# Triangular solve's scalings on VectorE, the root's product in another bank, and another order in the last slots

## The chip, the cores and the metric

The program runs on one core of one Trainium2 chip. TensorE multiplies matrices, VectorE, ScalarE and GpSimd work element by element, and SyncE issues transfers. The engines run side by side, each in its own order, and wait for one another on semaphores. The metric is device time in microseconds, lower is better. The kernel before took 1187.59 us, the median of three runs (1184.17, 1188.15, 1187.59).

## The reference

One decoder layer on 32 sequences of 64 tokens, 256 wide: a gated delta-rule attention over 128 steps per sequence (two keys for each token, 8 heads of 128), a cross attention with 16 heads and a window of 8 keys, and a gated feed-forward net of 1024 with weights stored as integers. After each comes a layer norm of the sum.

```
x = layernorm(x + delta_attention(x))      # 8 heads, T = 2 * 64 steps
x = layernorm(x + cross_attention(x, ctx, seg_id))
x = layernorm(x + ffn(x))                  # weights (w_int - 128) * scale

def step(state, inp):                      # the delta rule
    q_t, k_t, v_t, g_t, b_t = inp
    state = state * exp(g_t)
    corr = einsum('bhk,bhkv->bhv', k_t, state)
    v_new = (v_t - corr) * b_t
    state = state + einsum('bhk,bhv->bhkv', k_t, v_new)
    return state, einsum('bhk,bhkv->bhv', q_t, state)
o = o * rsqrt(mean(o * o) + EPS) * o_norm_w * silu(gg)
```

The kernel does not step through the 128 states. It builds the matrix of decayed products of the keys and solves a unit triangular system, in blocks of 32 rows.

## The kernel before

**Two phases.** `delta_phase` computes the first attention up to the gated heads; `tile_phase` does everything behind it, on 16 tiles of 128 tokens. Each engine has one program, written out in its order of execution; nothing reorders it.

**The delta phase** has 32 units (a head and a group of 8 sequences; U = 32) and runs in slots s = 0 to 42. It is a pipeline: slot s projects and convolves keys and queries of unit s, V and the gate of unit s - 9 (LAG = 9), makes the output of unit s - 10 and norms unit s - 11. From slot 32 on no new keys come; from slot 37 on parts of the tile phase stand between the slots' own work (`ahead[...]`), `last_slot` is 40.

**The solve** goes in 8 batches of 4 units (NS = 4). VectorE loads the 32x32 blocks (`solve_load`, `solve_norms`), GpSimd scales the rows by rho (L1396), runs 30 elimination steps of two instructions each (`eliminate`, L1328 and L1331), sets the diagonal and scales the columns (L1400, L1402), and VectorE turns the result (`solve_turn`, L1161, and `solve_turn_again`, L1165). The steps are cut up over four slots by the tables CUTS and LAST_CUTS: each slot has three pieces, ahead of and behind W_scaled and at the slot's end. X is the tile called `inverse`, rank_one the product of a step. The last batch, number 7, is eliminated in slots 33 to 36, and slot 37 is the first to need it.

**A slot's chain.** TensorE: `chain_y` (L628), V's first projection, the root's product `norm` (L724), `chain_inverse_low` (L638), `turn_v` (L534), V's second projection, the chain's high and low products (L664, L666; L651, L687 apart in the last slots), the gate's projection, `chain_sum_low` (L677), `output` (L552). ScalarE copies W (L947), GpSimd multiplies it by the key's norms (W_scaled, L1426), and `output` needs that. `less_sum` (L1191) on VectorE follows `chain_sum_low`; the next `chain_y` needs it. `norm` writes the mean of squares into bank VB, and `turn_v` writes V turned into the same bank; ScalarE takes the logarithm and the exponential (L989, L992).

**The seam.** The first tiles' work: `out` (w_out, L1571), first norm (`sums`, `normalize`: L1811 to L1818, L1839), `turn_x1` (L1580), query products, `scores` (L1620) with the turned queries that SyncE moves 16 pieces at a time (L1535), softmax (L1853 to L1864), `attT` (L1656), the mix with kvtok (L1678), ctxT copies (L1775) and w_uvo (L1691), second norm, `ffn` (L1632), down product (L1701). w_up is unpacked on VectorE (L1886), w_down on GpSimd (L1936, L1938). `span` runs s = 2 to 19, with tile u1 = s in its first part, s - 1 in scores, s - 2 in the cross attention's end, s - 3 in the feed-forward net and s - 4 in the last norm.

## Time and profile before

| | |
|---|---|
| profiled execution | 1185.69 us, span 1183.9 us, mean granted clock of TensorE 0.987 |
| busy | TensorE 1118.0 (94%), VectorE 819.6 (69%), ScalarE 704.7 (60%), GpSimd 517.7 (44%) |
| chain that ended last | TensorE 74%, VectorE 9%, GpSimd 7%, ScalarE 4% |

| stretch, us | TensorE busy | VectorE | ScalarE | GpSimd | granted clock |
|---|---|---|---|---|---|
| 620 to 640 (slot 33) | 14.19 | 12.57 | 10.81 | 11.07 | 0.83 |
| 640 to 660 | 19.22 | 14.57 | 17.60 | 16.31 | 1.00 |
| 660 to 680 (slots 36, 37) | 16.09 | 13.01 | 13.99 | 14.94 | 0.98 |
| 760 to 780 | 15.09 | 12.21 | 10.91 | 7.75 | 0.91 |
| 780 to 800 (the seam) | 15.79 | 15.24 | 4.76 | 5.92 | 0.91 |
| 800 to 1130 (steady tiles) | 329.14 | 199.21 | 147.59 | 32.50 | 1.00 |

A stretch's busy time is read against its length: 20 us in all rows but the last, 330 there. The granted clock is the share of TensorE's full 2.4 GHz; 0.5 is 1.2 GHz. Slots 33 to 37 start on TensorE at 617.8, 636.0, 649.1, 662.2 and 677.6 us.

### The profile page before, as it was taken

The page shows a single profiled execution, that of the slowest core. Times are in us where ns is not written, and L with a number is a line of the kernel's source. Part 1 is how long each engine was busy: PE and PEld are TensorE (multiplying, and loading weights), DVE is VectorE, ACT ScalarE, POOL GpSimd, SP SyncE. Part 2 cuts the span into 40 slices and gives each one's busy share as a digit, 9 for nine tenths or more (in the row PEclk, how much of TensorE's full clock was granted, in tenths as well). Part 3 has the DMA queues.
Part 4 walks back from the last instruction along what each step waited for, and adds up shares of the span by engine and source line. Part 5 has one row for each costly group of instructions (what it writes and reads, how often), then busy time and mean ns, then how long its engine had stood idle before and what let it go on. Part 6 is the DMA issues. An engine that isn't in the chain of part 4 may idle for free.

```text
span 1183.9 us, 28721 instructions
## 1 busy us (share of the span) xinstructions
PE 1118.0 (94%) x11460; PEld 772.8 (65%) x11460; DVE 819.6 (69%) x1447; ACT 704.7 (60%) x1214; POOL 517.7 (44%) x717
## 2 busy tenths in 40 slices
PE   8887899999999999999998899879999999999997
PEld 3444455555555555555555566668999899989976
DVE  5997778868868778779776655666556666565552
ACT  5776567777676776776766766534443444444443
POOL 1659486585784883983976712241100000010000
PEclk9999899999999999999998999989999999999999
DMA  4223234555545454565645542331222211112100
GB/s 122 49 51 81 69 51 79 87 106 74 115 79 92 95 78 89 113 123 116 127 75 167 160 129 64 113 102 46 50 51 52 68 52 46 46 45 51 30 16 9
DMA packets 147284, 93.74 MB, mean 79 GB/s; under 512 B 80688, under 2 KB 130736, under 8 KB 146256
## 3 DMA queue, kind: packets, MB, share of 16 engines
q1 hardware_dynamic: 146000, 91.71, 35.2%
q8 instruction: 91, 1.49, 0.5%
q14 instruction: 41, 0.34, 0.1%
q10 hardware_dynamic: 1152, 0.21, 0.1%
HBM read 54.77 MB, written 14.55 MB: 59 GB/s over the span
## 4 chain that ended last, share of the span: by engine, by line
PE 74%; DVE 9%; POOL 7%; ACT 4%; issue 3%; SPq 1%; DMA 1%; ACTq 0%; DVEq 0%; POOLq 0%
PE proj L528 21%; PE out L1632 5%; PE turned_v_chain L1632 5%; PE gram L543 5%; PE turned_v_chain L1701 4%; PE proj L1691 4%; PE proj L1571 4%; DVE conv L1114 3%; POOL inverse L1331 3%; PE gram L1606 2%; POOL rank_one L1328 2%; PE out L552 2%; PE turned_v_chain L534 2%; PE decays L559 2%; PE turned_v_chain L677 1%
## 5 line engine op out<-in xcount | busy, mean ns | idle before, releaser
L1114 DVE SCALAR_TENSOR_TENSOR conv<-proj,kq_weights,conv 128x504 f32<-128x504 f32 (+2 forms) x261 | 189.7, 732 | 30.4 <-ACT conv L843 24.0
L528 PE MATMUL proj<-xT,vg_weights 128*128 128x512 f32 x384 | 190.9, 621 | 2.2 <-DVE conv L1114 2.0
L1930 POOL TENSOR_TENSOR rope<-rope_part,rope_part 128x512 f32<-128x512 f32 x32 | 40.0, 1271 | 319.1 <-DVE rope_part L1871 319.1
L1114 DVE SCALAR_TENSOR_TENSOR conv<-proj,vg_weights,conv 128x504 f32<-128x504 f32 (+2 forms) x192 | 140.7, 733 | 45.2 <-ACT conv L843 40.1
L528 PE MATMUL proj<-xT,kq_weights 128*128 128x512 f32 x348 | 167.6, 608 | 0.2 <-DVE conv L1114 0.2
L1331 POOL TENSOR_TENSOR inverse<-inverse,rank_one 128x30 f32<-128x30 f32 (+14 forms) x240 | 126.5, 527 | 18.8
L1328 POOL TENSOR_TENSOR rank_one<-inverse 128x30 f32<-128x30 f32 (+14 forms) x240 | 116.8, 487 | 15.0
L528 PEld LDWEIGHTS proj<-xT,vg_weights 128*128 128x128 f32 x384 | 68.9, 193 | 66.5 <-issue 60.4
L528 PEld LDWEIGHTS proj<-xT,kq_weights 128*128 128x128 f32 x348 | 62.7, 191 | 74.8 <-issue 69.1
L843 ACT ACTIVATE conv<-proj,kq_weights 128x512 f32<-128x512 f32 x87 | 59.6, 687 | 54.6 <-PE proj L528 54.4
L1710 ACT ACTIVATE rstd<-rstd 128x1 f32<-128x1 f32 x48 | 9.7, 202 | 136.1 <-DVE rstd L1818 136.1
L543 PEld LDWEIGHTS gram<-keys_q 128*64 128x64 f32 x896 | 56.8, 136 | 51.8 <-ACT keys_q L854 33.5
L543 PE MATMUL gram<-keys_q 128*64 128x160 f32 (+2 forms) x896 | 73.4, 293 | 9.4 <-ACT keys_q L854 9.4
L854 ACT ACTIVATE keys_q<-conv 128x512 f32<-128x512 f32 x96 | 63.4, 667 | 16.9 <-DVE conv L1114 16.2
L843 ACT ACTIVATE conv<-proj,vg_weights 128x512 f32<-128x512 f32 x64 | 43.9, 685 | 41.7 <-PE proj L528 41.5
L1691 PE MATMUL proj<-t_w_uvo,ctxT 128*128 128x256 f32 x256 | 59.4, 386 | 2.7 <-ACT ctxT L1775 2.7
L1426 POOL TENSOR_TENSOR W_scaled<-W,k_norm 128x512 f32<-128x512 f32 x32 | 35.3, 1104 | 54.6 <-ACT W L947 54.6
L1701 PE MATMUL turned_v_chain<-t_w_down,hid 128*128 128x256 f32 x256 | 58.0, 379 | 0.9 <-DVE hid L1878 0.9
L1435 POOL TENSOR_TENSOR o_sum<-o_sum,q_sq 128x512 f32<-128x512 f32 x23 | 29.5, 1283 | 64.2 <-ACT o_sum L1046 64.2
L1176 DVE COPY Y<-turned_v_chain 32x256 f32<-32x256 f32 x64 | 27.1, 424 | 41.1 <-PE turned_v_chain L628 39.6
L1691 PEld LDWEIGHTS proj<-t_w_uvo,ctxT 128*128 128x128 f32 x256 | 48.5, 194 | 9.7 <-issue 3.5
L1701 PEld LDWEIGHTS turned_v_chain<-t_w_down,hid 128*128 128x128 f32 x256 | 48.6, 190 | 7.7 <-DVE hid L1878 1.1
(257 smaller groups left out, 2487.6 us busy)
## 6 DMA issues: line engine op xcount, KB each, us to landing
kq_weights<-in_kq_w SPq DMA_DIRECT2D x32, 390.0 KB, 6.5
vg_weights<-in_vg_w SPq DMA_DIRECT2D x32, 390.0 KB, 6.2
o_scratch<-oT SPq DMA_DIRECT2D x32, 256.0 KB, 2.2
o_in<-o_scratch SPq DMA_DIRECT2D x16, 512.0 KB, 4.0
o_rs<-o_rs_quarters SPq DMA_DIRECT2D x88, 64.0 KB, 6.1
diagonal<-gram_decayed SPq DMA_DIRECT2D x128, 32.0 KB, 1.9
inverse<-inverse SPq DMA_DIRECT2D x32, 128.0 KB, 2.8
q_first<-rope SPq DMA_DIRECT2D x128, 32.0 KB, 1.9
```

The lines of the kernel that those rows point to most:

```text
L528: mm = e.matmul(bank(c, u)[:], w[:, (k * 3 + c % 3) * 128:(k * 3 + c % 3 + 1) * 128], xT[g][:, k, :], start=(k == 0), stop=(k == KD - 1))
L543: mm = e.matmul(out[p, b % 4, cols], kq[:, b, S:][:, p], kq[:, b, cols], start=True, stop=True)
L843: e.activation(acc(c, u)[:], bank(c, u)[:].rearrange("p (b l) -> p b l", l=S), ACT.Copy, scale=weights(c, u)[:, j:j + 1]).then_inc(s_tap[c ...
L854: e.activation(out, acc(c, u)[:], ACT.Silu).then_inc(s_silu[c], 1)
L1114: e.scalar_tensor_tensor(acc(c, u)[:, :, back:], src[:, :, 0:S - back], weights(c, u)[:, j:j + 1], acc(c, u)[:, :, back:], ALU.mult, ALU.a ...
L1328: e.tensor_tensor(product, X[:, k + 1:, k:k + 1].broadcast_to([128, n, k]), X[:, k:k + 1, 0:k].broadcast_to([128, n, k]), ALU.mult).then_i ...
L1331: e.tensor_tensor(X[:, k + 1:, 0:k], X[:, k + 1:, 0:k], product, ALU.add).then_inc(s_elim, 1)
L1571: mm = e.matmul(out_bank(u)[:, 0:D], o_in[u % 2][:, h, :], w_out[:, h, :], start=(h == 0), stop=(h == H - 1))
L1632: mm = e.matmul(ffn_bank[r][:, (2 * i + j) * TILE:(2 * i + j + 1) * TILE], wt[:, k, (2 * r + j) * 128:(2 * r + j + 1) * 128], x2T[:, k, :] ...
L1691: mm = e.matmul(b0[:, 0:D], ctxT[:, hp].rearrange("p b q -> p (b q)"), w_uvo[:, hp, :], start=(hp == 0), stop=(hp == XH // 2 - 1))
L1701: mm = e.matmul(b6[:, 0:D], hid[:, k, :], w_down[:, k, :], start=(k == 0), stop=(k == FJ - 1))
L1930: e.tensor_tensor(turned[half][:].rearrange("p b r q -> p r b q"), parts[2 * half][:], parts[2 * half + 1][:], op).then_inc(s_turned, 1)
```

## The change

In the delta phase: (1) the last batch's rows are scaled by VectorE, right behind its norms in slot 33, and its columns (with the memset of the diagonal) by VectorE in slot 36, right ahead of `solve_turn`. (2) GpSimd takes W_scaled first in slots 32 to 36 and the steps behind it, in pieces of 11, 8 and 11 (LAST_CUTS); batch 6's column scaling too comes behind W_scaled in slot 32. (3) For units 22 to 29 the root's product goes into bank P[1], which the second projections of V use: `norm` waits for the convolution that read it, V's projection for the logarithm, and `turn_v` no longer.

In the tile phase: (4) each transfer of integers has a semaphore of its own, w_up is unpacked ahead of the second norm of tile 0, w_down by VectorE in one instruction in the next step, instead of two on GpSimd. (5) At the seam (u3 == 0) ScalarE copies ctxT ahead of the queries and VectorE does tile 1's softmax sum behind the second norm. (6) In the last slots ScalarE copies x2T ahead of the last norm's root. (7) The down product starts when three of hid's four parts are there and waits for the fourth ahead of its seventh of eight pieces.

```diff
-LAST_CUTS = (((1, 1), (5, 13), (1, 5)), ((13, 13), (13, 21), (21, 21)), ((21, 21), (21, 31), (31, 31)), ((31, 31), (31, 31), (31, 31)))
+LAST_CUTS = ((1, 12), (12, 20), (20, 31), (31, 31))
...
+        in_v_bank = lambda u: by_rows(u) or u + LAG + 2 > last_slot
...
                     else:
-                        mm = e.matmul(VB, ones_mean[:], o_sum[:], start=True, stop=True)
+                        if not in_v_bank(u):
+                            e.wait_ge(s_conv[V1], 3 * (u + 2))
+                        mm = e.matmul(VB if in_v_bank(u) else P[1][:], ones_mean[:], o_sum[:], start=True, stop=True)
                     mm.then_inc(s_norm, 1)
...
                     if live(ud):
                         e.wait_ge(s_silu[V1], ud + 1)
-                        wait(e, s_ln, ud)
+                        if in_v_bank(ud - 1):
+                            wait(e, s_ln, ud)
...
                             e.wait_ge(s_conv[Q], 3 * (ub + 1))
                         else:
                             e.wait_ge(s_conv[V1], 3 * uc)
+                        if not in_v_bank(uc - 2):
+                            e.wait_ge(s_ln, uc - 1)
                         project(V1, uc)
...
                             e.wait_ge(s_gr, uo)
-                            o_ln, o_mean = o_rs[:], VB
+                            o_ln, o_mean = o_rs[:], VB if in_v_bank(uo) else P[1][:]
                         e.activation(o_ln, o_mean, ACT.Ln, scale=float(2 ** O_SHIFT), bias=guard[:, 0:1]).then_inc(s_ln, 1)
...
 
+                def solve_scale_rows(h):
+                    e.wait_ge(s_solve, SOLVE * h + READY)
+                    e.tensor_tensor(X, X, rho[:, :, None].broadcast_to([128, RB, RB]), ALU.mult).then_inc(s_elim, 1)
+
+                def solve_scale_columns(h):
+                    e.wait_ge(s_elim, ELIM * h + ELIM - 2)
+                    e.memset(padded[:, 0:RB * RB:RB + 1], 1.0).then_inc(s_elim, 1)
+                    e.wait_ge(s_elim, ELIM * h + ELIM - 1)
+                    e.tensor_tensor(X, X, rho[:, None, :].broadcast_to([128, RB, RB]), ALU.mult).then_inc(s_elim, 1)
...
                         solve_norms(loading)
+                        solve_scale_rows(loading)
...
                     if turning is not None and s > U:
+                        solve_scale_columns(turning)
                         solve_turn(turning)
...
                     solving = 0 <= h < NB_SOLVE
-                    cuts = (LAST_CUTS if h == NB_SOLVE - 1 else CUTS)[cut]
+                    cuts = ((1, 1), LAST_CUTS[cut], (1, 1)) if h == NB_SOLVE - 1 else CUTS[cut]
...
                     elif solving:
-                        if cut == 0 and s > U:
-                            scale_rows()
-                            eliminate(h, cuts[2])
                         eliminate(h, cuts[0])
-                        if cut == 3 and s <= U:
+                        if cut == 3 and s < U:
                             scale_columns()
                     if live(ud):
...
                                         ALU.mult).then_inc(s_wk, 1)
                     if solving and h > 0:
                         eliminate(h, cuts[1])
-                        if cut == 3 and s > U:
+                        if cut == 3 and s == U:
                             scale_columns()
                     if live(ud) and s <= U:
...
                         e.tensor_tensor(oT[uo % 2][:], oT[uo % 2][:], o_rs[:], ALU.mult).then_inc(s_gr, 1)
-                    if solving and h > 0 and not (cut == 0 and s > U):
-                        if cut == 0:
+                    if solving and h > 0:
+                        if cut == 0 and s < U:
                             scale_rows()
                         eliminate(h, cuts[2])
...
                             mm.then_inc(s_cross, 1)
                         if live(u4):
-                            e.wait_ge(s_hid, 4 * (u4 + 1))
+                            e.wait_ge(s_hid, 4 * u4 + 3)
                             if u4 == 0:
-                                e.wait_ge(s_down_w, 2)
+                                e.wait_ge(s_down_w, 1)
                             wait(e, s_parts, 4 * (u1 + 1) if live(u1) else 0)
                             wait(e, s_norm[2], 5 * u4 - 4)
                             for k in range(FJ):
+                                if k == FJ - 2:
+                                    e.wait_ge(s_hid, 4 * (u4 + 1))
                                 mm = e.matmul(b6[:, 0:D], hid[:, k, :], w_down[:, k, :], start=(k == 0), stop=(k == FJ - 1))
                             mm.then_inc(s_down, 1)
...
                         u1, u2, u3, u4, u5 = s, s - 1, s - 2, s - 3, s - 4
-                        if live(u5):
+                        if live(u5) and live(u1):
...
                             e.activation(x2T[:], b5[:, 0:KD * TILE].rearrange("p (k n) -> p k n", k=KD), ACT.Copy).then_inc(s_x2tout, 1)
+                        if live(u5) and not live(u1):
+                            rsqrt(2, u5)
                         if live(u1):
                             copy_x1(u1)
...
-                        if live(u1):
+                        if live(u1) and u3 != 0:
                             copy_nope(u1)
...
                             e.wait_ge(s_mix, u3 + 1)
                             wait(e, s_cross, u3)
                             for b, bk in enumerate((b1, b2)):
                                 e.activation(ctxT[:, :, b, :], bk.rearrange("p (h q) -> p h q", q=S), ACT.Copy).then_inc(s_ctx, 1)
+                        if u3 == 0:
+                            copy_nope(u1)
                         if live(u4):
...
                     if n == "w_up":
-                        e.wait_ge(done["ints"], 32)
+                        e.wait_ge(done["up"], 16)
...
+
+                def unpack_down():
+                    e.wait_ge(done["scales"], 64)
+                    e.wait_ge(done["down"], 16)
+                    e.scalar_tensor_tensor(w_down[:], ints["w_down"][:], -ZERO_POINT, scales["w_down"][:, None, :].broadcast_to([128, FJ, D]),
+                                           ALU.add, ALU.mult).then_inc(s_down_w, 1)
...
+                        if s == AHEAD:
+                            dequantize("w_up")
+                        if s == AHEAD + 1:
+                            unpack_down()
                         if live(u4):
                             hidden(2, u4)
                             hidden(3, u4)
...
-                        if live(u2):
+                        if live(u2) and u3 != 0:
                             softmax_sum(u2)
                         if u3 == 0:
                             e.wait_ge(done["scaled"], U)
                         if live(u3):
                             sums(1, u3)
                             normalize(1, u3)
-                        if s == AHEAD:
-                            dequantize("w_up")
+                        if u3 == 0:
+                            softmax_sum(u2)
                         if live(u1):
...
-                def unpack_down():
-                    e.wait_ge(done["scales"], 64)
-                    e.wait_ge(done["ints"], 32)
-                    e.tensor_scalar(w_down[:], ints["w_down"][:], -ZERO_POINT, None, ALU.add).then_inc(s_down_w, 1)
```

GpSimd, slots 32 and 33, from behind batch 6's last step (`inverse` is the solve's tile). Before:

```order
L1400 MEMSET inverse 128x32
L1402 TENSOR_TENSOR inverse<-inverse,rho 128x1024
L1426 TENSOR_TENSOR W_scaled<-W_125,k_norm_143 128x512
L1435 TENSOR_TENSOR o_sum<-o_sum,q_sq_113 128x512
L1442 TENSOR_TENSOR oT_145<-oT_145,o_rs 128x512
L1396 TENSOR_TENSOR inverse<-inverse,rho 128x1024
L1328 TENSOR_TENSOR rank_one<-inverse 128x30
L1331 TENSOR_TENSOR inverse<-inverse,rank_one 128x30
```

After:

```order
L1441 TENSOR_TENSOR W_scaled<-W_125,k_norm_143 128x512
L1418 MEMSET inverse 128x32
L1420 TENSOR_TENSOR inverse<-inverse,rho 128x1024
L1450 TENSOR_TENSOR o_sum<-o_sum,q_sq_113 128x512
L1457 TENSOR_TENSOR oT_145<-oT_145,o_rs 128x512
L1441 TENSOR_TENSOR W_scaled<-W_126,k_norm_143 128x512
L1346 TENSOR_TENSOR rank_one<-inverse 128x30
L1349 TENSOR_TENSOR inverse<-inverse,rank_one 128x30
```

W_scaled of both slots has moved up, ahead of the column scaling and ahead of the last batch's first step; the row scaling has left GpSimd.

VectorE, slot 33, from the end of the last batch's norms to the sum of squares (`kq_decayed` is less_sum's, `oT` first gate_output's, then scale_output's). Before:

```order
L1154 MEMSET inverse 128x16
L1114 SCALAR_TENSOR_TENSOR conv_87<-proj,vg_weights_84,conv_87 128x8x63
L1114 SCALAR_TENSOR_TENSOR conv_87<-proj,vg_weights_84,conv_87 128x8x62
L1114 SCALAR_TENSOR_TENSOR conv_87<-proj,vg_weights_84,conv_87 128x8x61
L1249 SCALAR_TENSOR_TENSOR oT_144<-out,o_norm_w,gate_132 128x512
L1186 TENSOR_TENSOR oT_144<-oT_144,o_rs 128x512
L1191 TENSOR_TENSOR kq_decayed_71<-kq_decayed_71,turned_v_chain 64x8x32
L1181 TENSOR_TENSOR o_sum<-o_sum,q_sq_114 128x512
```

After:

```order
L1160 MEMSET inverse 128x16
L1164 TENSOR_TENSOR inverse<-inverse,rho 128x1024
L1120 SCALAR_TENSOR_TENSOR conv_87<-proj,vg_weights_84,conv_87 128x8x63
L1120 SCALAR_TENSOR_TENSOR conv_87<-proj,vg_weights_84,conv_87 128x8x62
L1120 SCALAR_TENSOR_TENSOR conv_87<-proj,vg_weights_84,conv_87 128x8x61
L1265 SCALAR_TENSOR_TENSOR oT_144<-out,o_norm_w,gate_132 128x512
L1202 TENSOR_TENSOR oT_144<-oT_144,o_rs 128x512
L1207 TENSOR_TENSOR kq_decayed_71<-kq_decayed_71,turned_v_chain 64x8x32
L1197 TENSOR_TENSOR o_sum<-o_sum,q_sq_114 128x512
```

One instruction of 128x1024 has come in, and all that follows stands behind it.

VectorE at the seam, from the last of rope_parts(2) to the unpacking of w_up or the masks (`total` is softmax_sum(1), `res`, `stats`, `mv`, `rstd` and `x` the second norm of tile 0). Before:

```order
L1871 TENSOR_TENSOR rope_part_200<-proj,t_cos_149 128x512
L1860 TENSOR_REDUCE total<-att_206 128x16
L1862 RECIPROCAL total<-total 128x16
L1864 TENSOR_TENSOR att_206<-att_206,total 128x1024
L1811 TENSOR_TENSOR res_184<-proj,x_0_175 128x256
L1813 BN_STATS stats_187<-res_184 128x6
L1815 BN_AGGR mv_190<-stats_187 128x2
L1818 TENSOR_SCALAR rstd_193<-mv_190 128x1
L1839 TENSOR_SCALAR x_0_178<-res_184,mv_190,rstd_193 128x256
L1886 SCALAR_TENSOR_TENSOR t_w_up<-w_up_ints,w_up_scale 128x1024 x2
L1800 TENSOR_TENSOR mask_173<-t_keys,seg 128x128
```

After:

```order
L1892 TENSOR_TENSOR rope_part_200<-proj,t_cos_149 128x512
L1907 SCALAR_TENSOR_TENSOR t_w_up<-w_up_ints,w_up_scale 128x1024 x2
L1832 TENSOR_TENSOR res_184<-proj,x_0_175 128x256
L1834 BN_STATS stats_187<-res_184 128x6
L1836 BN_AGGR mv_190<-stats_187 128x2
L1839 TENSOR_SCALAR rstd_193<-mv_190 128x1
L1860 TENSOR_SCALAR x_0_178<-res_184,mv_190,rstd_193 128x256
L1881 TENSOR_REDUCE total<-att_206 128x16
L1883 RECIPROCAL total<-total 128x16
L1885 TENSOR_TENSOR att_206<-att_206,total 128x1024
L1821 TENSOR_TENSOR mask_173<-t_keys,seg 128x128
```

w_up's unpacking has moved from behind the second norm to ahead of it, softmax_sum from ahead to behind.

## Rows read from the trace of the kernel before

**Rows 1.** Timeline of PE, slots 33 and 37: start, length (us), operation, idle before.
```profile
634.14 1.98 PE L552 MATMUL out<-W_scaled,V 128*64 128x64 f32 x32 [5.18 <-POOL W_scaled L1426]
...
677.57 0.69 PE L628 MATMUL turned_v_chain<-inverse,gram_decayed 32*32 32x32 f32 x32 [2.57 <-DVE inverse L1161]
```

**Rows 2.** Groups of POOL, 629.5 to 671.8 us: busy, mean ns | idle before.
```profile
L1331 POOL TENSOR_TENSOR inverse<-inverse,rank_one 128x30 f32<-128x30 f32 (+14 forms) x30 | 17.8, 593 | 2.4
L1328 POOL TENSOR_TENSOR rank_one<-inverse 128x30 f32<-128x30 f32 (+14 forms) x30 | 14.9, 498 | 2.1
L1426 POOL TENSOR_TENSOR W_scaled<-W,k_norm 128x512 f32<-128x512 f32 x4 | 4.2, 1041 | 2.0 <-ACT W L947 2.0
L1396 POOL TENSOR_TENSOR inverse<-inverse,rho 128x1024 f32<-128x1024 f32 x1 | 1.9, 1914 | 7.6 <-DVE inverse L1154 7.6
```

**Rows 3.** Timeline of POOL: the scaling of the columns, last batch.
```profile
672.87 2.60 POOL L1402 TENSOR_TENSOR inverse<-inverse,rho 128x1024 f32<-128x1024 f32 x1
```

**Rows 4.** Timeline of ACT: the copy of W in slot 32.
```profile
612.47 0.59 ACT L947 ACTIVATE W<-turned_v_chain 64x512 f32<-64x512 f32 x1
```

**Rows 5.** Timeline of DVE, slots 32 and 33.
```profile
614.99 2.05 DVE L1161 STREAM_TRANSPOSE inverse<-inverse 128x1024 f32<-128x1024 f32 x1
617.92 0.69 DVE L1127 TENSOR_TENSOR gram_decayed<-gram,decayed 128x512 f32<-128x512 f32 x1 [0.88 <-PE gram L543]
...
631.07 0.41 DVE L1191 TENSOR_TENSOR kq_decayed<-kq_decayed,turned_v_chain 64x256 f32<-64x256 f32 x1
```

**Rows 6.** Groups of DVE by shape: busy, mean ns | idle before.
```profile
L1864 DVE TENSOR_TENSOR att<-att,total 128x1024 f32<-128x1024 f32 x16 | 20.0, 1248 | 0.6
```

**Rows 7.** Queue of SyncE; DMA issues of 636 to 639 us (KB, us to landing).
```profile
638.14 0.39 SPq L449 DMA_DIRECT2D vg_weights<-in_vg_w  x1
...
vg_weights<-in_vg_w SPq DMA_DIRECT2D x1, 390.0 KB, 6.9
```

**Rows 8.** Waits, 600 to 830 us: us in total, times, longest.
```profile
PE turned_v_chain L534 <- ACT o_rs L989: 4.1, 8, 1.2
```

**Rows 9.** Timeline of PE at the seam, 775 to 792 us.
```profile
775.30 5.13 PE L1691 MATMUL proj<-t_w_uvo,ctxT 128*128 128x256 f32 x16 [2.66 <-ACT ctxT L1775]
...
784.80 0.69 PE L1620 MATMUL proj<-t_kE,q_first 128*64 128x64 f32 x16
...
791.59 0.47 PE L1580 MATMUL turned_v_chain<-ident,x 128*128 128x128 f32 x2 [3.46 <-DVE x L1839]
791.86 1.91 PE L1632 MATMUL out<-x2T,t_w_gate 128*128 128x128 f32 x8
```

**Rows 10.** Timeline of ACT at the seam: the first copy of ctxT.
```profile
774.11 0.60 ACT L1775 ACTIVATE ctxT<-proj 128x512 f32<-128x512 f32 x1
```

**Rows 11.** Tile q_second on SyncE: issue ns, first and last start, landing.
```profile
L1535 SPq DMA_DIRECT2D q_second<-rope x8: 596/597/602, 773.3 to 782.2; - x8
...
DMA to landing us min/median/max: 1.9/1.9/2.4
```

**Rows 12.** Timeline of DVE at the seam.
```profile
777.60 1.22 DVE L1860 TENSOR_REDUCE total<-att 128x16 f32<-128x1024 f32 x1 [5.25 <-ACT att L1734]
...
782.45 3.70 DVE L1839 TENSOR_SCALAR x<-res,mv,rstd 128x256 f32<-128x256 f32 x1 [0.51 <-ACT rstd L1712]
786.07 2.35 DVE L1886 SCALAR_TENSOR_TENSOR t_w_up<-w_up_ints,w_up_scale 128x1024 f32<-128x1024 int32 x2
```

**Rows 13.** Timeline of POOL at the seam.
```profile
781.47 4.53 POOL L1938 TENSOR_TENSOR t_w_down<-t_w_down,w_down_scale 128x2048 f32<-128x2048 f32 x1
```

**Rows 14.** Waits, 1100 to 1184 us.
```profile
PE out L1632 <- ACT x2T L1752: 2.5, 2, 1.9
...
PE turned_v_chain L1701 <- DVE hid L1878: 0.9, 1, 0.9
```

**Rows 15.** Timeline of PE: L1606 with a wait inside it, and without.
```profile
711.87 2.19 PE L1606 MATMUL gram<-qc,t_w_qn 96*128 96x128 f32 x16
...
769.66 1.95 PE L1606 MATMUL gram<-qc,t_w_qn 96*128 96x128 f32 x16
```

More of the change, by code:

```diff
@@ L244, in delta_phase @@
             "const", "in", "kv_stored", "stored", "rope_stored", "product", "copied", "rope"))
-        d_w, d_ints, d_uvo, s_wgt = sem("d_weights"), sem("d_ints"), sem("d_w_uvo"), sem("ffn_weights")
+        d_w, d_up, d_down, d_uvo, s_wgt = sem("d_weights"), sem("d_up"), sem("d_down"), sem("d_w_uvo"), sem("ffn_weights")
         d_gate = sem("d_gate_weights")
@@ L412, in weights_after_chain @@
                     e.dma_start(tiles["w_uvo"][:], scratch["w_uvo"]).then_inc(d_uvo, 16)
-                    for n, k in (("w_up", "up"), ("w_down", "down")):
-                        e.dma_start(ints[n][:].rearrange("p k n -> p (k n)"), a[f"{k}_w"]).then_inc(d_ints, 16)
+                    for n, k, landed in (("w_up", "up", d_up), ("w_down", "down", d_down)):
+                        e.dma_start(ints[n][:].rearrange("p k n -> p (k n)"), a[f"{k}_w"]).then_inc(landed, 16)
                 def gate_weights():
@@ L1455, in delta_phase @@
     tiles["ints"], tiles["scales"] = ints, scales
-    done = {"o": s_og, "w_high": s_whiout, "scaled": s_gr, "stored": d_out, "weights": d_w, "first": d_first, "uvo": d_uvo, "ffn": s_wgt, "ints": d_ints, "scales": d_gate, "decays": s_ee,
+    done = {"o": s_og, "w_high": s_whiout, "scaled": s_gr, "stored": d_out, "weights": d_w, "first": d_first, "uvo": d_uvo, "ffn": s_wgt, "up": d_up, "down": d_down, "scales": d_gate, "decays": s_ee,
             "gram": s_gm, "gate": s_silu[G], "v1": s_conv[V1], "high": s_wlo, "low": s_wloout, "solve": s_solve}
@@ L1931, in rope @@
                                         parts[2 * half + 1][:], op).then_inc(s_turned, 1)
-                def unpack_down():
-                    e.wait_ge(done["scales"], 64)
-                    e.wait_ge(done["ints"], 32)
-                    e.tensor_scalar(w_down[:], ints["w_down"][:], -ZERO_POINT, None, ALU.add).then_inc(s_down_w, 1)
-                    e.wait_ge(s_down_w, 1)
-                    e.tensor_tensor(w_down[:], w_down[:], scales["w_down"][:, None, :].broadcast_to([128, FJ, D]),
-                                    ALU.mult).then_inc(s_down_w, 1)
                 def loop():
```

2 lines of the change are left out of this document (removed).

## The prediction

> **What bounds the kernel now.** I read the page first: its busy digits put TensorE at nine tenths or more almost everywhere, and the chain that ended last is TensorE for 74%. From 800 us on, where the tiles run in a steady state, the matmuls leave no gap. So nothing in this change can help there; it can help only where TensorE stands still, and the list of waits and then the timelines say where that is. There are four such places, and all of them are touched.
>
> First, slots 33 to 37, the last batch of the triangular solve. In slot 33 TensorE waits 5.18 us in front of `output(23)` for GpSimd's W_scaled, and at the head of slot 37 2.57 us for the inverse that VectorE turns [rows 1]. These are one matter. GpSimd's queue holds the last batch's work in a row: the scaling of the rows (1.9 us), 60 elimination instructions (14.9 + 17.8 us busy and 2.4 + 2.1 us between them, 37.2 us together), four W_scaled of 1.04 us among them, one wait of 2.0 us for W [rows 2], and at the end the scaling of the columns, 2.6 us [rows 3]. That is 1.9 + 37.2 + 4.2 + 2.0 + 2.6 = 47.9 us, with 0.2 for a memset 48.1. TensorE's work in those slots is shorter than that, so this chain, not TensorE, sets the time at which slot 37 starts. The 5.18 us wait is not worth 5.18 us: it is slack against that chain.
>
> Second, the root's product in the bank of the turned V: turn_v waits for ScalarE's logarithm 8 times, 4.1 us in all [rows 8]. Third, the seam at 775 to 792 us: 2.66 us for ctxT and 3.46 us for x, with a matmul group at half clock behind each [rows 9]. Fourth, the last slots: 2.5 us for x2T and 0.9 us for hid [rows 14].
>
> **Term 1, the solve chain: 2.4 us.** Slot 32: W_scaled now stands in front of batch 6's column scaling. W is copied until 612.47 + 0.59 = 613.06 [rows 4], so W_scaled ends at 614.1 and memset and scaling (0.2 + 2.6) end at 616.9. VectorE's turn of the inverse moves from 614.99 to 616.9; it had 0.88 us to spare behind it [rows 5], so everything later on VectorE in slots 32 and 33, the loading of the last batch included, is 1.0 us late. TensorE no longer waits for W_scaled there, but then waits for the inverse, so that gain is not kept.
>
> Slot 33: the scaling of the rows moves to VectorE, right behind the norms. An operation of 128x1024 with both inputs in SBUF takes VectorE 1.25 us where nothing disturbs it [rows 6]. W_scaled(23) is ready at just that time and GpSimd, now idle, runs it. What happens when both want SBUF is to be seen at the seam: the normalization that starts at 782.45 on VectorE takes 3.70 us [rows 12] and ends with GpSimd's operation, 781.47 + 4.53 = 786.00 [rows 13]. So I count a hold of one whole W_scaled: 1.04 + 1.25 = 2.3 us until step 1 can start; without a hold it is 1.3. The same at the end: when step 30 is done GpSimd takes up W_scaled(26) at once, VectorE is held for 1.04, then needs 1.25 and 0.1 for the memset: 2.4 us instead of 2.8, or 1.4 without the hold.
>
> The Trainium skill (SBUF — State Buffer, "Who interferes with whom") says that a VectorE instruction with two SBUF inputs contends with a GpSimd instruction that reads SBUF, and that whichever starts first keeps the pair of ports for its whole length. By that rule both scalings are held, as counted; if only the form seen at the seam, with one tensor input, were held, the sum would be 2.1 us better. The trace agrees with the hold at the seam; for two tensor inputs of the scaling's size no row here settles it.
>
> The new chain: start 1.0 later, 2.3 for the rows, 37.2 of steps, only two W_scaled (24 and 25) inside it = 2.1, a wait for W, and 2.4 for the columns. The wait: `less_sum(24)` stands behind the row scaling on VectorE, at 631.07 before [rows 5], now at 631.1 + 1.0 + 2.3 = 634.4, and `chain_y(25)`, the head of slot 34, needs it. TensorE would have reached output(23) at 634.14 - 5.18 = 629.0 [rows 1]; 1.0 later and with the product's 1.1 it is at chain_y at about 631, so the 5.18 us wait comes back as some 3.6 us in front of chain_y. Slot 34 then starts at 634.8, against 634.14 + 1.9 = 636.0 before. W(24) had kept GpSimd waiting for 2.0 us [rows 2] when it stood behind twelve steps; it comes 1.2 us earlier now, the eleven steps ahead of it end about as late as eleven steps did before, and W_scaled(23), 1.04, has left the queue: estimated, W(24) is some 0.7 us late. Sum: 1.0 + 2.3 + 37.2 + 2.1 + 0.7 + 2.4 = 45.7, against 48.1: 2.4 us. On SyncE the store of unit 22's output waits for VectorE's scale_output, which is as late as less_sum; behind it stand nine loads and then the weights of unit 26, issued at 638.14 and landed 6.9 us later [rows 7]. Now that is 641.4 and 648.3; slot 35, one slot of 12 us behind 634.8, wants them at about 647.3. I count that within the 0.7. Bounds: no hold and no wait for W, 5.2 us; a wait for W of 3 us (late weights, TensorE at half clock), 0.
>
> **Term 2, the bank: 0.4 us.** The wait for the logarithm moves from turn_v(0) to `project(V1)`, one group of four transposes (some 0.5 us) later. At most that in each of 7 slots. But turn_v(1), behind V1, waits for ScalarE's copy of V, which comes after the same logarithm and its exponential: where the root waits were long (slots 38 to 40), V1 then ends earlier and TensorE waits for the copy instead. In slots 34 to 36 term 1's chain is the limit. I keep 0.2 us each in slots 37 and 39; bounds 0 and 2. `norm` gets a wait for V1's convolution of the slot before; in the order of VectorE's queue that is long done.
>
> **Term 3, the seam: 4.1 us.** ctxT's copies go ahead of the four copies of q. The product before ended at 775.30 - 2.66 = 772.64 [rows 9], the first copy started at 774.11 [rows 10]: 1.4 us earlier, so the w_uvo product ends at 780.4 - 1.4 = 779.0 or sooner. On VectorE w_up's unpacking (2.35 us [rows 12]) moves into its idle time before 777.60, where it waited 5.25 us; softmax_sum moves behind the second norm; GpSimd's two w_down operations are gone, and with them the hold (3.70 instead of about 0.4: 3.3 us). VectorE then: product end 779.0, second norm 2.4 (780.43 to 782.45 and the last operation), softmax_sum 2.7, mask and next first norm 3.2 (788.4 to 791.59): 787.3, when x1 is ready. TensorE: scores(2) need the stores of the turned queries; the last is issued at 782.2 and lands 1.9 later [rows 11], 784.1, and this path is not changed. From scores to turn_x1 it was 784.80 to 791.59 - 3.46 = 788.1, 3.3 us: 787.4. So turn_x1 at 787.5 instead of 791.59. Without the early w_uvo product the floor by TensorE's row stays the same; if VectorE is 1.5 late, 2.6 us are left; the stores cap it at 4.2. w_down's unpacking, 128x2048 in one operation, costs VectorE about 2.35 us (like w_up's two) in front of hidden(2), where VectorE otherwise waits for ScalarE: nothing. If that cover were gone, up to 2.35 us would be late in hidden(2), and by that the down product.
>
> **Term 4, the end: 3.1 us.** x2T goes ahead of the last root. Of 2.5 us of waits in two slots [rows 14], the longer, 1.9, keeps the copy itself, 0.4; the shorter is covered by the transposes of att: 2.1. The down product starts when three quarters of hid are there: the last one waits 0.9 us for the fourth, and six of its eight parts now fill that: 0.9; with the waits unrounded 3.1. Bounds 2.5 and 3.4.
>
> **Term 5, the clock: 1.7 us.** After the seam's 3.46 us wait the granted clock is the lower of its two levels: the first group of eight matmuls behind it takes 1.91 us [rows 9]. At the upper level half of that would do, and the next group is nearly as slow: some 1.7 us lost; behind the 2.57 us wait of slot 37 [rows 1] it fell too, and I count as much. The waits that I expect at these places are 1 to 1.5 us in slot 37 and some 2 us (for the stores) at the seam. I take one low stretch of two away: 1.7, bounds -1.7 (a new one, in slot 34 or 35) and 3.4.
>
> **The sum.** 2.4 + 0.4 + 4.1 + 3.1 + 1.7 = 11.7 us. The profiled execution took 1185.69 us (span 1183.9): 1174.0. The median of the runs is 1187.59, 1.9 above it: 1175.9, say 1176.
>
> **The rivals.**
> (a) The solve chain gives nothing back: late weights and a low clock in slot 34 put W(24) and W(25) behind the steps, and no low stretch vanishes. For it: four things are queued behind the row scaling on VectorE and SyncE. Against: the chain drops two W_scaled and a 2.0 us wait. 0.4 + 4.1 + 3.1 = 7.6 us less: 1180.0.
> (b) No hold on VectorE, no wait for W, both low stretches gone: 5.2 + 0.4 + 4.1 + 3.1 + 3.4 = 16.2 us less: 1171.4. Against it: GpSimd's W_scaled does coincide with both scalings.
> (c) Slower: the wait that now stands inside the down product, ahead of part 7 of 8, breaks TensorE's stream in each of 16 tiles, 13 of them steady. The trace has one such place: 16 matmuls with a wait in the middle took 2.19 us, without 1.95 [rows 15]. At 0.24 it costs 16 x 0.24 = 3.8, which leaves 7.9: 1179.7. It makes the kernel slower by over 0.3% from (11.7 + 3.6) / 16 = 0.96 us each; at 1.1 us each it is 17.6 - 11.7 = 5.9 us slower, 1193.5. For that, four times the only price seen would be needed.
> (d) The moved order only trades waits, slots 33 to 37 losing 4 by a longer chain and the seam gaining 1 because VectorE waits for w_up's load: 3.1 + 1 + 0.4 - 4 = 0.5 us less: 1187.1, within the noise.
>
> **Chances.** The forecast 0.54 (its own range 1173 to 1179), (a) 0.18, (b) 0.15, (c) at its small price 0.04 and at its large one 0.04, (d) 0.05. About 0.3% (3.6 us) is what a measurement of this kernel can tell from no change. Faster 0.91, same 0.05, slower 0.04. The range, 1170 to 1182, holds the forecast, nearly all of (b) and most of (a).
>
> **What would show it.** Term 1: W_scaled(23) right behind its W; a wait of 3 to 4 us at the head of slot 34 for less_sum; VectorE's scaling of 128x1024 at about 2.3 us rather than 1.25; slot 37 starting 2.4 us earlier. Term 3: x at 0.4 us, scores(2) waiting for q_second, turn_x1 some 4 us earlier relative to slot 42. Term 4: no wait for hid, x2T's wait 0.4. Term 5: one low stretch less. I am wrong if slot 37 starts over 5 us earlier or not earlier, or if a steady tile takes longer than before.

## The result and the profile after

The changed kernel takes 1176.84 us (median of 8 runs, 1172.62 to 1181.99), the kernel before 1186.37 (median of 8, its first three among them). The ratio is 0.9926, 95% interval 0.9902 to 0.9949. Timed again later it was 0.9923 (0.9911 to 0.9935). So it is faster by 9 us, in a range of 6 to 12. The profiled execution has a span of 1173.4 us, 10.5 less than before.

The stretches of the two programs are best compared by their own length, with these borders on TensorE: head of slot 32 (`chain_y(23)`), slot 37 (`chain_y(28)`), slot 38, the transposes of att of slot 41, where the seam begins, `down_q(3)` of the seam, and the last down product. First the kernel before (stretch in us, length, busy time and count of PE, PEld, DVE, ACT, POOL, mean granted clock, DMA share, GB/s):

```profile
602.74:677.59 74.85, 63.32 (x980) 39.66 (x976) 51.28 (x79) 54.15 (x87) 56.34 (x91) 0.95 0.55 147
677.59:696.40 18.81, 18.32 (x234) 11.30 (x234) 11.54 (x22) 9.54 (x16) 1.57 (x2) 0.91 0.66 185
696.40:764.77 68.37, 60.88 (x922) 43.48 (x921) 40.83 (x68) 45.11 (x76) 16.30 (x13) 1.00 0.22 58
764.77:795.28 30.51, 22.80 (x182) 19.05 (x180) 23.34 (x32) 10.17 (x19) 13.24 (x5) 0.89 0.46 162
795.28:1175.72 380.44, 375.26 (x3268) 338.26 (x3267) 218.88 (x472) 169.16 (x345) 32.50 (x26) 1.00 0.17 43
```

The same five stretches in the first profile of the changed kernel:

```profile
600.37:674.15 73.78, 65.09 (x978) 39.39 (x974) 53.81 (x82) 53.09 (x87) 51.80 (x88) 0.95 0.55 149
674.15:691.85 17.70, 16.67 (x232) 10.98 (x232) 12.40 (x22) 10.46 (x17) 2.31 (x3) 1.00 0.61 173
691.85:762.37 70.52, 64.18 (x921) 45.17 (x921) 41.83 (x68) 45.14 (x76) 17.19 (x13) 0.95 0.26 76
762.37:788.31 25.94, 20.93 (x182) 17.90 (x179) 19.72 (x31) 10.06 (x19) 3.49 (x2) 0.93 0.46 154
788.31:1165.33 377.02, 374.82 (x3268) 338.52 (x3267) 221.08 (x473) 168.58 (x344) 34.58 (x26) 1.00 0.17 44
```

The gains are 1.07, 1.11, -2.15, 4.57 and 3.42 us, and 2.37 come from ahead of slot 32 (602.74 against 600.37), where nothing was changed; together 10.4. The third stretch is longer although its waits are not: its clock is 0.95 where it was 1.00. 0.05 x 70.5 = 3.5 us of lost clock is one stretch of 7 us at half clock. The seam has less of it than before, 0.93 against 0.89. What belongs to the program and what to the execution can't be told from two profiles; the runs below tell part of it.

Slots 33 to 37 on TensorE, to be read beside [rows 1]:

```profile
630.98 1.16 PE L553 MATMUL out<-W_scaled,V 128*64 128x64 f32 x32 [2.38 <-DVE oT L1265]
...
671.00 1.15 PE L553 MATMUL out<-W_scaled,V 128*64 128x64 f32 x32 [1.82 <-POOL W_scaled L1441]
...
674.15 0.69 PE L629 MATMUL turned_v_chain<-inverse,gram_decayed 32*32 32x32 f32 x32 [0.99 <-DVE inverse L1177]
```

The wait of 5.18 us for W_scaled is 2.38 now, and it is for VectorE: `gate_output` stands behind the row scaling and the V1 convolution and frees the bank that `output(23)` writes. The size is this execution's; in the second profile of the same kernel the wait is 3.64 us. GpSimd in the same slots:

```profile
627.13 1.76 POOL L1441 TENSOR_TENSOR W_scaled<-W,k_norm 128x512 f32<-128x512 f32 x1 [10.30 <-ACT W L953]
...
643.17 1.52 POOL L1441 TENSOR_TENSOR W_scaled<-W,k_norm 128x512 f32<-128x512 f32 x1 [1.81 <-ACT W L953]
...
669.90 1.04 POOL L1441 TENSOR_TENSOR W_scaled<-W,k_norm 128x512 f32<-128x512 f32 x1
```

and VectorE's two scalings with the turn:

```profile
626.76 1.23 DVE L1164 TENSOR_TENSOR inverse<-inverse,rho 128x1024 f32<-128x1024 f32 x1
...
670.16 1.86 DVE L1170 TENSOR_TENSOR inverse<-inverse,rho 128x1024 f32<-128x1024 f32 x1
672.06 2.04 DVE L1177 STREAM_TRANSPOSE inverse<-inverse 128x1024 f32<-128x1024 f32 x1
```

The seam on TensorE answers to [rows 9]; the last line shows that the wait for x is gone:

```profile
771.30 3.69 PE L1706 MATMUL proj<-t_w_uvo,ctxT 128*128 128x256 f32 x16 [1.25 <-ACT ctxT L1794]
...
781.61 0.69 PE L1635 MATMUL proj<-t_kE,q_first 128*64 128x64 f32 x16 [2.29 <-DMA q_second<-rope]
...
786.31 0.38 PE L1595 MATMUL turned_v_chain<-ident,x 128*128 128x128 f32 x2
```

At the end, of the waits in [rows 14] one of 0.5 us is left, and hid is gone from the list:

```profile
PE out L1647 <- ACT x2T L1769: 0.5, 1, 0.5
```

### The profile page after: what moved, and what is told of

Read it like the earlier page. It is cut to its first block, busy times and chain, and to the rows that moved or that the text cites. A ratio compares the mean times of both kernels' runs of the same rounds, so it can differ in the third digit from the quotient of the medians.

```text
span 1173.4 us, 28728 instructions
## 1 busy us (share of the span) xinstructions
PE 1118.5 (95%) x11460; PEld 774.2 (66%) x11460; DVE 822.9 (70%) x1451; ACT 704.7 (60%) x1214; POOL 507.1 (43%) x712
## 4 chain that ended last, share of the span: by engine, by line
PE 76%; DVE 9%; POOL 5%; ACT 3%; issue 3%; SPq 2%; DMA 1%; ACTq 0%; DVEq 0%; POOLq 0%
PE proj L529 21%; PE out L1647 5%; PE gram L544 5%; PE turned_v_chain L1647 5%; PE turned_v_chain L1718 4%; PE proj L1706 4%; PE proj L1586 4%; DVE conv L1120 3%; PE gram L1621 2%; PE out L553 2%; PE turned_v_chain L535 2%; POOL inverse L1349 2%; PE decays L560 2%; POOL rank_one L1346 2%; SPq L1550 2%
## 5 line engine op out<-in xcount | busy, mean ns | idle before, releaser
L1120 DVE SCALAR_TENSOR_TENSOR conv<-proj,kq_weights,conv 128x504 f32<-128x504 f32 (+2 forms) x261 | 189.7, 732 | 30.1 <-ACT conv L849 23.7
L1961 POOL TENSOR_TENSOR rope<-rope_part,rope_part 128x512 f32<-128x512 f32 x32 | 43.1, 1367 | 324.7 <-DVE rope_part L1892 324.7
```

The costliest lines, as they stand in the source:

```text
L1120: e.scalar_tensor_tensor(acc(c, u)[:, :, back:], src[:, :, 0:S - back], weights(c, u)[:, j:j + 1], acc(c, u)[:, :, back:], ALU.mult, ALU.a ...
L1961: e.tensor_tensor(turned[half][:].rearrange("p b r q -> p r b q"), parts[2 * half][:], parts[2 * half + 1][:], op).then_inc(s_turned, 1)
```

## The experiments

Each ratio is taken against the kernel before on the same chip; e9 to e12 ran on another chip than e1 to e8. In the rows of stretches below the borders lie up to 0.7 us behind the named instructions, by the same amount at all borders of one profile, so the lengths are those from instruction to instruction.

**Each part of the change alone.** Four kernels, each the kernel before with one part of the diff and nothing else.

```diff
e1: -LAST_CUTS = (((1, 1), (5, 13), (1, 5)), ...   +LAST_CUTS = ((1, 12), (12, 20), (20, 31), (31, 31))
    +solve_scale_rows(loading)   +solve_scale_columns(turning)   (VectorE; gone from GpSimd)
e2: -e.matmul(VB, ones_mean[:], o_sum[:]   +e.matmul(VB if in_v_bank(u) else P[1][:], ...   (with its waits)
e3: +if u3 == 0: copy_nope(u1)   +if u3 == 0: softmax_sum(u2)   +unpack_down() on VectorE, w_up's earlier
e4: +if live(u5) and not live(u1): rsqrt(2, u5)   +if k == FJ - 2: e.wait_ge(s_hid, 4 * (u4 + 1))
```

> Before with only the last batch's part: both scalings on VectorE, GpSimd's steps behind the scaled W in cuts (1,12), (12,20), (20,31). My theory, read from the trace after: GpSimd's 30 steps stay one chain with one wait for W(24) inside (1.8 us) and the scaled W(26) ahead of the column scaling, so slot 37 starts only 1.1 us nearer to slot 32 than before, and slot 37 gets 1 us more by running at full clock: 2.2 us less in all, ratio 0.998. Rival, as I predicted: 2.4 from the chain and 1.7 from the clock, 4.1 less, 0.9965. Rival 2: nothing, the waits are only moved, 1.000.

> Before with only the root's product in P[1]. My theory: the wait for Ln goes, but the same turn waits for the V copy right behind it, so 0 to 0.4 us less: ratio 0.9997 to 1.000. Rival: the full gap of eight waits, 2 us less, 0.998.

> Before with only the seam's part: ctxT copied ahead of the copy, softmax_sum behind the normalizing, both feed-forward weights unpacked on VectorE in other places, two semaphores. My theory: mix to turn_x1(3) 2.7 us shorter and the feed-forward of tile 2 at full clock, 1.7: 4.4 less, ratio 0.9963. Rival: the wait for the unpacked w_down was hidden by the stores, 1 us less or nothing, 0.999.

> Before with only the end's part: x2T copied ahead of the root in the last slots, and the wait for the last quarter of hid inside the down product. My theory: 2.0 us of x2T's wait and 0.9 us of hid's at the end go, nothing is lost in the 15 steady tiles: 3 us less, ratio 0.9975. Rival: a wait inside the accumulation costs 0.24 us in each of 16 tiles, then 0.8 more, 1.0007.

Measured against before: e1 0.9986 (0.9971 to 1.0), e2 1.0004 (0.9992 to 1.0016), e3 0.9974 (0.9963 to 0.9984), e4 0.9957 (0.9942 to 0.9972). In us that is -1.7, +0.5, -3.1 and -5.1, in sum -9.4, as much as the whole change within the intervals. Clear of no change are the seam and the end; e1's interval ends at 1.0 and e2's holds it. The stretches show what each part does. Seam alone, fourth and fifth stretch:

```profile
765.00:791.13 26.13, 21.13 (x181) 17.87 (x180) 19.89 (x32) 10.35 (x20) 2.97 (x3) 0.93 0.53 183
791.13:1173.18 382.05, 376.88 (x3266) 339.86 (x3266) 221.15 (x473) 169.45 (x345) 34.60 (x26) 1.00 0.17 43
```

The seam is 4.4 us shorter than in the first profile of before, as in the whole change (but only 2.5 shorter than in the second, see below; the timed runs give 3.1); the tail of this execution lost 1.6 to a stretch at half clock at 1164. End alone, all stretches but the first:

```profile
678.05:695.19 17.14, 16.66 (x244) 10.96 (x238) 11.18 (x22) 9.92 (x16) 1.94 (x2) 1.00 0.63 189
695.19:765.99 70.80, 63.31 (x912) 45.11 (x905) 42.10 (x69) 44.77 (x76) 16.79 (x13) 0.95 0.27 75
765.99:793.43 27.44, 22.57 (x181) 18.47 (x180) 17.95 (x31) 10.37 (x20) 13.36 (x4) 0.88 0.42 141
793.43:1170.44 377.01, 374.82 (x3266) 338.23 (x3265) 219.48 (x472) 168.60 (x344) 32.53 (x26) 1.00 0.17 44
```

Its last stretch has the full 3.4 us of the end. But up to 793 us this kernel is the kernel before, and still slot 37 is 1.7 us shorter at full clock, the third stretch 2.4 longer and the seam 3.1 shorter at much the same clock. No edit did that. The bank alone makes the third stretch 68.09 instead of 68.37, 0.28 us, and slot 37 18.57 instead of 18.81, 0.24 us, and the timed runs see nothing of it. The solve part alone:

```profile
602.93:678.62 75.69, 64.87 (x986) 39.43 (x981) 55.90 (x83) 53.21 (x87) 50.98 (x88) 0.95 0.54 145
```

Slot 37 starts 0.84 us later against slot 32, not 1.1 earlier as I read from the trace after. The row scaling was held here (GpSimd's W_scaled kept it waiting), `output(23)` waited 3.64 us for VectorE, and a new wait stands behind it on TensorE:

```profile
650.21 2.62 PE L528 MATMUL proj<-xT,vg_weights 128*128 128x512 f32 x4 [1.70 <-DMA vg_weights<-in_vg_w]
```

with the load issued at 641.60 and 8.6 us on its way. The store of oT that SyncE has ahead of it waits for VectorE. GpSimd then waited 2.86 and 1.84 us for W(24) and W(25), in place of one wait of 2.0 [rows 2].

**The order in slots 33 and 34.** Four kernels on top of the change.

```diff
e5: -LAST_CUTS = ((1, 12), (12, 20), (20, 31), (31, 31))   +LAST_CUTS = ((1, 13), (13, 21), (21, 31), (31, 31))
e6: solve_scale_rows(loading); +gate_output(); +scale_output(uo); +less_sum(uc); convolve(V1, uc)
e7: SyncE: -if s == U + 1: weights_after_keys()   +the same in slot U + 2, behind the vg weights
e8: e6 and e7 together
```

> After with one more elimination step in slot 33, LAST_CUTS (1,13), (13,21), (21,31). My theory: GpSimd waits 1.8 us for W(24) in slot 34 with nothing in hand; a step of 1.3 us fits in there, so its chain and slot 37 come 1.0 to 1.3 us earlier against slot 32: ratio to before 0.9915 where after had 0.9926. Rival: the step makes the scaled W(24) late and TensorE loses what the chain gains, as after, 0.9926.

> After with gate_output, scale_output and less_sum directly behind the row scaling in slot 33, ahead of the V1 convolution. My theory: TensorE's wait for oT (2.38 us there) falls to under 0.5, chain_y(25) starts 1.5 to 2 us earlier, the store of oT and with it SP's queue too, so the weights of unit 26 land 1.5 us earlier, W(24) as well: slot 37 starts 1 to 2 us nearer to slot 32, ratio 0.9913. Rival: V1's convolution is late by the 1.8 us that was put ahead of it and the turned V of slot 34 waits for it: no change, 0.9926.

> After with SP's nine loads for the tile phase moved from slot 33 behind the load of the weights of unit 26 in slot 34. They are not wanted before slot 38. My theory: the late scaled oT holds SP's store and the eleven issues behind it; without them the weights are issued some 4.5 us earlier, TensorE's stop of 0.9 us at the head of slot 35 goes, slot 35 starts 0.9 earlier, and slot 37 gets part of it: 0.5 to 0.9 us, ratio 0.992. Rival: GpSimd's elimination alone sets slot 37, the stop of 0.9 goes but nothing is gained at slot 37, 0.9926.

> After with both of the last two edits. My theory: no stop of TensorE over 0.5 us from slot 33 to 35, and GpSimd waits for W(24) no more, since W comes 2 us earlier: its chain of 30 steps ends 1.5 to 2 us nearer to its start, slot 37 with it, ratio 0.991. Rival: GpSimd's chain is as long as before, whatever TensorE does, 0.9926.

Measured against before: e5 0.9916 (0.9899 to 0.9934), e6 0.9951 (0.9933 to 0.9969), e7 0.994 (0.9921 to 0.996), e8 0.9947 (0.9924 to 0.9971). From slot 32 to 37 they took 74.00, 76.32, 75.37 and 72.69 us (after 73.78). All four intervals against before overlap that of the changed kernel, so none of the four is shown to be faster or slower than it; what follows is read from the profiles. e5's theory, slot 37 1.0 us earlier, isn't borne out: `output(23)` waited 4.44 us for VectorE in this execution, W(24) came later by it, and the wait for it is still 1.75 us. e6's theory fell: the wait for oT became 1.47 us, and a stop of 2.74 us for the gate came, which ScalarE writes behind the V1 convolution that now ends later:

```profile
635.92 3.75 PE L529 MATMUL proj<-xT,vg_weights 128*128 128x512 f32 x4 [2.74 <-ACT gate L958]
```

So my rival was right in kind: VectorE is full in slot 33, and what goes first there makes something else late. e7's fell too: the weights are issued at 636.72 and land 3.7 us later instead of 7.5, yet the stop at the head of slot 35 is 0.70 us (0.93 and 0.66 in the two profiles of the changed kernel). Late weights were the wait in e1 but not that one; what it is stays open. e8's theory, no stop over 0.5 us and no wait for W(24), fell as well: TensorE stopped 2.54 us for the gate, and GpSimd waited 0.82 us. It is also a lesson in profiles: its profiled execution is the fastest of all (1172.09 us, clock 0.98 in the first stretch), and its median is 1180.65.

**Waits inside the product, a better order, and both kernels again.**

```diff
e9:  -e.wait_ge(s_hid, 4 * u4 + 3)      +e.wait_ge(s_hid, 4 * u4 + 1)
     -if k == FJ - 2: e.wait_ge(s_hid, 4 * (u4 + 1))
     +if k > 0 and k % 2 == 0: e.wait_ge(s_hid, 4 * u4 + k // 2 + 1)
e10: slot 33: +gate_output() ahead of solve_load(loading, 0); less_sum ahead of scale_output; and e7's edit
```

> After with the down product waiting for hid four times in each of the 16 tiles, ahead of its first, third, fifth and seventh step, where after waits ahead of the first and the seventh: 32 more waits inside the accumulation, and the two of them already fulfilled in the steady tiles. My theory: a wait that is already fulfilled costs nothing there; tile period 26.21 us as before, ratio as after, 0.9926. Rival: each costs 0.12 us or more, then 4 us more in all, 0.996, and a period of 26.45.

> After with gate_output of slot 33 ahead of the load of the diagonal (VectorE waits there 0.4 to 0.9 us for the DMA), less_sum ahead of scale_output, and SP's nine loads behind the weights of unit 26. My theory: output(23) waits for the scaled W alone, the V1 convolution is no later, chain_y(25) starts 1 to 1.4 us earlier against slot 32, and W(24) with it; slot 37 gets 1.0 to 1.4 us: ratio 0.9915. Rival: VectorE is full in slot 33 and TensorE stops for the gate behind the V1 convolution in place of oT; no gain, 0.9926.

> The changed kernel once more, unaltered, to see what a second profile and six more times of the same program show. My theory: the 2.3 us that its first profile was ahead of before already at 600 us are the run's, not the change's, so this profile is level with before there within 1 us, and the stretches at half clock lie elsewhere: span about 1176, ratio 0.9926 to 0.995. Rival: the lead ahead of slot 32 is the program's and stands here too, 2.3 us.

> The kernel before once more, unaltered, for a second profile of it. My theory: the number and the places of the half-clock stretches between 640 and 800 us differ from the first profile's, by one stretch of 3.4 us or more, although the program is the same. Rival: they lie in the same places, and what I saw move between kernels was moved by the edits. Ratio 1.000 either way.

Measured against before: e9 0.9941 (0.992 to 0.9962), e10 0.9911 (0.9898 to 0.9924), after again 0.9923, before again 1.0002 (0.9987 to 1.0017). e9's last stretch, with 32 more waits:

```profile
796.09:1173.09 377.00, 374.81 (x3268) 338.39 (x3267) 220.93 (x473) 168.47 (x344) 34.55 (x26) 1.00 0.17 44
```

377.00 us as without them (377.02): a wait that is already fulfilled costs nothing measurable inside the accumulation. From 800 to 1130 us the down product's matmuls take 379 ns each before, in the changed kernel and in e9. The ratio of e9 isn't told apart from that of after again; its profiled execution, 1182.70 us, is its slowest, at a clock of 0.91, 0.84 and 0.93 in the first three stretches. Up to slot 37 its code is that of the changed kernel, and yet:

```profile
602.91:680.15 77.24, 67.14 (x981) 41.38 (x976) 55.06 (x83) 52.93 (x87) 50.88 (x88) 0.91 0.54 143
```

```profile
647.78 1.52 POOL L1441 TENSOR_TENSOR W_scaled<-W,k_norm 128x512 f32<-128x512 f32 x1 [4.96 <-ACT W L953]
```

From 632 to 647 us, in slots 33 and 34, the granted clock was 0.67 (0.89 in the first profile after), and GpSimd waited 4.96 us for W(24), where it had waited 1.81. The changed kernel again:

```profile
602.64:676.72 74.08, 63.72 (x982) 38.97 (x980) 54.16 (x82) 53.17 (x87) 51.12 (x88) 0.98 0.56 149
676.72:693.59 16.87, 16.76 (x241) 10.89 (x238) 11.42 (x22) 10.48 (x17) 2.93 (x3) 1.00 0.63 185
693.59:761.68 68.09, 61.74 (x921) 43.52 (x918) 40.94 (x68) 44.99 (x76) 16.31 (x13) 1.00 0.24 65
761.68:787.78 26.10, 21.10 (x180) 17.86 (x180) 19.72 (x32) 10.16 (x19) 3.21 (x3) 0.93 0.54 186
787.78:1164.78 377.00, 374.82 (x3268) 338.40 (x3267) 220.96 (x473) 168.49 (x343) 34.55 (x26) 1.00 0.17 44
```

The same program starts slot 32 at 602.5, where before had 602.7: the lead of 2.37 us was the first execution's. It has no half clock in the third stretch, which is 68.09 us against 70.52. The kernel before again started slot 32 at 600.7, and its half clock at the seam was one piece, on the w_uvo product, and not two:

```profile
762.76:791.35 28.59, 22.73 (x181) 18.49 (x179) 19.87 (x31) 10.28 (x20) 12.91 (x5) 0.88 0.48 168
...
772.98 6.68 PE L1691 MATMUL proj<-t_w_uvo,ctxT 128*128 128x256 f32 x16 [2.66 <-ACT ctxT L1775]
```

28.59 us against 30.51 for one program. From turn_x1 to down_q it took 2.06 us, where the first profile took 3.68 at half clock. My expectation for it was half right: places moved, not the amount (0.11 x 30.51 and 0.12 x 28.59 are both 3.4 lost). e10 does in slot 33 what e6 was meant to do: `output(23)` waits no more, `chain_y(25)` waits 2.13 us for less_sum, the gate 0.25, GpSimd 1.15 for W(24). Its stretches 1 and 4:

```profile
601.69:674.53 72.84, 63.80 (x986) 38.63 (x980) 53.22 (x82) 53.09 (x87) 51.65 (x88) 0.98 0.56 151
...
762.87:787.47 24.60, 19.60 (x181) 16.62 (x180) 19.46 (x31) 10.26 (x20) 3.48 (x2) 1.00 0.43 145
```

It is 1.2 us shorter than after again up to slot 37 at the same clock, in one profile each. Its seam has no half clock, but the stretch ahead of it does (71.46 us at 0.93, against 68.09 at 1.00 in after again). Its median, 1173.58, is 0.9 below that of after in the same runs. It beats the kernel before; against the changed kernel the intervals overlap.

## Why the prediction was right, and where it was not

1176 us was forecast and 1176.84 measured (1174.49 the second time). The number is nearer than the mechanism earns: 11.7 us less was forecast, and the ratios give 9. The forecast went from 1187.59, the median of three runs of the kernel before; the median of eight is 1.2 lower. The first profile gives 10.5, of which 2.4 are not the change's. Term by term:

| term | forecast, us less | shown, us less (-: more) | from |
|---|---|---|---|
| 1 solve chain | 2.4 | 1.1, 0.8, -0.8 and -2.4 | 74.85 to 73.78, 74.08, 75.69 (e1) and 77.24 (e9) |
| 2 bank | 0.4 | 0.5 | 68.37 to 68.09 (e2, after again) and slot 37 in e2, 0.24 |
| 3 seam | 4.1 | 2.4 to 2.9 | att transposes of slot 41 to turn_x1(3): 26.83 and 26.54 to 23.94 and 24.09 |
| 4 end | 3.1 | 3.4 | 380.44 to 377.0, in e4 alone too |
| 5 clock | 1.7 | -1.4 to 3.4 | slot 37, the stretch behind it and the seam, see below |

**Term 1 is the step that failed in size.** Four profiled executions have this order up to slot 37, and they took 73.78 to 77.24 us; five without it (before, before again, e2, e3, e4) took 74.55 to 74.89. So no profile shows 2.4 us, two show a loss, and the timed e1 gives 1.7 us, with 0 and 3.4 as its bounds, slot 37's clock included. In the first profile the pieces ahead of the failed step held: the inverse of slot 32 was 1.0 us late (the head of slot 33, 617.8 and 616.5, is 15.1 us behind that of slot 32 before and 16.1 after), GpSimd's first step came 1.6 later against slot 32 (1.4 forecast), and the weights of unit 26 were issued at 639.05, which is 641.4 less the lead of 2.35. What failed is "W(24) is some 0.7 us late": GpSimd waited 1.81 us, 2.85 in the second profile. I had let eleven steps end as late as eleven did before, but before there were twelve in front of that W; the twelfth, 1.3 us, now runs behind the wait. With it the wait is 2.0 and the term 1.1, as measured in that profile. In e9 the wait was 4.96 us, and that is beyond my bound of 3. The second error is my wait of 3.6 us at `chain_y(25)` for less_sum: the wait is one instruction earlier, at `output(23)`, for gate_output, which I had not followed to its bank. Its size, 2.38 us in the first profile, was 3.64 in the second and in e1.

**The holds.** I counted 1.04 us at each scaling. The row scaling took 1.23 us in the first profile, without a hold, because it started 0.37 us ahead of W_scaled; then W_scaled took 1.76 instead of 1.04. Where W_scaled was first the row scaling took 1.85:

```profile
627.93 1.04 POOL L1435 TENSOR_TENSOR W_scaled<-W,k_norm 128x512 f32<-128x512 f32 x1 [8.98 <-ACT W L947]
```

```profile
628.20 1.85 DVE L1158 TENSOR_TENSOR inverse<-inverse,rho 128x1024 f32<-128x1024 f32 x1
```

(both of e1). The first to start keeps its time and the other pays about what is left of it: 0.8 us were left here and 0.6 paid, also at the columns (1.86). Both have two inputs in SBUF. The operation that writes x at the seam, in the order before, shows it over four lengths: of GpSimd's w_down product 3.55, 1.82, 2.16 and 0.82 us were left when x started (before, before again, e1, e4), and x took 3.70, 1.97, 2.31 and 0.97 us, against 0.41 with GpSimd idle. The Trainium skill (SBUF — State Buffer, "Who interferes with whom") says that a VectorE instruction with two SBUF inputs contends with a GpSimd instruction that reads SBUF, and that the order of issue decides which of them blocks; these rows agree with it. My error was to take the whole of the other's length.

**Term 3.** The mechanism held: x takes 0.41 us, scores(2) waits for the stores of q_second (2.29 us), turn_x1 for nothing. A stretch at half clock from scores(2) on made the way to turn_x1 4.70 us where I had 3.3. In e9 and e10, without it, that way is 3.16 us and the whole path 22.59, 4.2 less than in the first profile of before, as forecast; but both had their half clock in the stretch ahead of the seam instead. Over all profiles the path is 26.3 us in the mean of the five without this order and 23.7 in the nine with it. The whole seam goes from 29.0 to 25.7, 3.3 less, near the 3.1 that e3 was timed at; terms 3 and 5 had 4.1 and up to 1.7 there.

**Term 4.** 3.42, at the upper bound.

**Term 5 can't be forecast as I did.** I tied one low stretch to each wait. At the seam that holds in part. Behind the wait of 2.66 us for ctxT the w_uvo product took 5.13 to 6.71 us in all five profiles without the seam's part, and behind 1.25 us it took 3.69 in all nine with it. But from turn_x1 to down_q, where I placed the loss, it is 2.0 us after, 3.68 in the first profile of before and in e2 (wait 3.46), and 2.06 in before again, e1 and e4, where the wait for x was 0.73 to 2.06 us: those 1.7 us were gone in three profiles without the edit. In slot 37 and behind scores(2) the same wait has either level: slot 37 is 17.14 us at clock 1.00 in e4 and 18.76 at 0.91 in e3, behind the same code and waits of 2.38 and 2.40 us, and the changed kernel lost 3.5 us of clock in its third stretch once and nothing the next time. Against the first profile of before, slot 37 (less 0.2 for the bank) and the clock make 0.9 - 2.4 (behind it) + 1.7 = 0.2 us in the first profile after and 1.7 + 0 + 1.7 = 3.4 in the second; against before again the last part is 0.1, and they make -1.4 and 1.8. My 1.7 lies among them, and that is luck. Why a stretch falls here in one execution and there in the next stays open.

**The rivals.** (a) did not win on the time, but for term 1 it named what e1 and e9 show: W(24) behind the steps in both, with a low clock in slot 34 in e9, and W(25) too in e1, behind late weights. (b) no: the median, and W_scaled held the columns in both profiles after and the rows in the second. (c) is shown wrong by the last stretch, which lost 3.4 us with the wait inside it, and by e9. (d) no: slots 32 to 36 lost 2.4 us at most, in e9, and the seam gained 2.5 us or more.

## What to carry to other kernels

A chain on one engine with waits in it is priced step by step behind each wait: a step moved from ahead of a wait to behind it is paid in full. Before an operation is put into a full engine's queue, follow every buffer that the operations behind it free, banks too. And where an effect is under 1%, compare stretches of equal granted clock and profile the same program more than twice; two single profiles gave 2.4 us that no edit had made, and slots 32 to 36 of one and the same code took 73.78, 74.08 and 77.24 us. Where a part's gain is of that size, only the timed runs can tell it, and for the solve part alone they leave it open.
